# Cross-attention of a decoder block on one core: tile-outer order, unrolled, output summed in PSUM, mask added by PE, rope partners by DMA, bf16 P times V

## The reference

```
kv_c = kv @ W_kvc;  q_c = q @ W_dq                      # 64 and 96 columns
q_nope = q_c @ W_uq;  q_rope = rope(q_c @ W_qr)          # 16 heads, 128 and 64
k_nope = kv_c @ W_uk; v = kv_c @ W_uv; k_rope = rope(kv_c @ W_kr)
scores = (q_nope . k_nope + q_rope . k_rope) * scale     # per head, 64 x 64
scores = where(seg_id - 8 <= key <= seg_id, scores, -1e30)
x = layernorm(x + softmax(scores) @ v @ W_o)
rope([x1, x2]) = [x1*cos - x2*sin, x1*sin + x2*cos]      # halves of 32 each
```

## Time and profile before

| | |
|---|---|
| median of 3 runs | 1627.86 us (1627.15 to 1629.86) |
| the profiled execution's own time | 1630.34 us |
| its span | 1628.5 us |
| PE, DVE, ACT, POOL busy, of the span | 91%, 81%, 82%, 76% |
| self-attention | 0 to about 970 us |
| preparation of the cross-attention | about 970 to 1049 us |
| cross-attention | 1049.0 (first projection) to 1450.9 us (end of the last addition to X) |
| feed-forward | to the end |
| instructions | 54216 |

### The profile page before, as it was taken

How to read it: one execution, slowest core, us unless ns; L and a number is a source line. 1 busy time by engine, 2 the same in 40 slices (tenths; PEclk the granted TensorE clock), 3 DMA queues, 4 the chain that set the end, 5 groups by cost and what they waited for, 6 DMA issues and landing times. The chain is left out here.

```text
span 1628.5 us, 54216 instructions
## 1 busy us (share of the span) xinstructions
PE 1487.4 (91%) x20018; PEld 1083.8 (67%) x20018; DVE 1322.9 (81%) x2913; ACT 1334.4 (82%) x4174; POOL 1231.7 (76%) x1147
## 2 busy tenths in 40 slices
PE   6998999999999999999999968799999999845996
PEld 3666777777777777777777755366666666633664
DVE  3887777777777777777777778699999999967986
ACT  5877888888888888888888856599999999976664
POOL 5999888888898898898898846466666666611787
PEclk9999999999999999999999978999999999976999
DMA  6700000000000000000000002200000000000011
GB/s 222 191 2 15 16 3 15 16 15 3 15 15 3 16 15 5 13 15 15 3 15 3 3 2 68 86 3 2 0 0 0 0 0 0 0 1 0 14 39 53
DMA packets 27066, 36.92 MB, mean 23 GB/s; under 512 B 8288, under 2 KB 19872, under 8 KB 26848
## 3 DMA queue, kind: packets, MB, share of 16 engines
q1 hardware_dynamic: 26848, 33.99, 6.6%
HBM read 29.79 MB, written 4.19 MB: 21 GB/s over the span
## 5 line engine op out<-in xcount | busy, mean ns | idle before, releaser
L420 DVE SCALAR_TENSOR_TENSOR X<-projP,r,X 128x256 f32<-128x256 f32 x512 | 211.3, 476 | 2.5 <-PE projP L254 2.4
L234 PEld LDWEIGHTS svP<-W,xT 128*128 128x128 bf16 x3072 | 182.7, 98 | 31.4 <-issue 1.4
L205 PE MATMUL qkssP<-xT,W 128*128 128x512 bf16 x768 | 190.4, 384 | 13.5 <-POOL W L485 11.1
L480 POOL TENSOR_TENSOR y_sql<-y_sq 128x512 bf16<-128x512 f32 x128 | 133.0, 1039 | 80.5 <-ACT y_sq L321 80.1
L234 PE MATMUL svP<-W,xT 128*128 128x128 bf16 x3072 | 192.9, 219 | 0.7 <-issue 0.7
L205 PE MATMUL kP<-xT,W 128*128 128x512 bf16 x768 | 188.4, 382 | 0.0
L254 PE MATMUL projP<-W,y 128*128 128x256 bf16 x1024 | 177.1, 275 | 3.2 <-POOL yl L480 3.2
L943 ACT ACTIVATE x_probs<-x_scores,x_ntop 128x64 f32<-128x64 f32 x512 | 170.0, 335 | 7.4 <-DVE x_ntop L985 7.4
L336 ACT ACTIVATE probs<-scores,ntop 128x64 f32<-128x64 f32 x512 | 170.5, 339 | 1.9 <-DVE ntop L410 1.9
L1008 POOL TENSOR_TENSOR x_probs<-x_probs,x_inv 128x512 f32<-128x512 f32 x64 | 66.7, 1042 | 107.9 <-DVE x_inv L968 107.9
L480 POOL TENSOR_TENSOR k_sql<-k_sq 128x512 bf16<-128x512 f32 x128 | 133.1, 1040 | 19.8 <-ACT k_sq L341 19.2
(11 more groups left out here) (190 smaller groups left out, 4829.1 us busy)
## 6 DMA issues: line engine op xcount, KB each, us to landing
w_stage<-in_wqkvp SPq DMA_DIRECT2D x16, 512.0 KB, 3.5
x_stage<-in_xT SPq DMA_DIRECT2D x8, 512.0 KB, 3.6
X<-in_x SPq DMA_DIRECT2D x1, 4096.0 KB, 17.2
x_stage<-in_ctxT SPq DMA_DIRECT2D x8, 512.0 KB, 3.6
out<-X SPq DMA_DIRECT2D x8, 512.0 KB, 2.9
okv<-in_L_xattn_W_o SPq DMA_DIRECT2D x1, 2048.0 KB, 11.7
okv<-in_wgT SPq DMA_DIRECT2D x1, 1024.0 KB, 4.9
okv<-in_wuT SPq DMA_DIRECT2D x1, 1024.0 KB, 7.2
```

Source lines behind the costliest of these rows:

```text
L205: last = nc.tensor.matmul(dst[:, :], weight(parity, u, i, c), xT[:, z, c, tok], start=(c == 0 and k == 0), stop=(c == CC - 1 and k == 2))
L234: last = nc.tensor.matmul(svP[:, b * D:(b + 1) * D], xT[:, u, c, t * TILE + b * P:t * TILE + (b + 1) * P], weight(parity, z, 2, c), start= ...
L420: last = nc.vector.scalar_tensor_tensor(acc, projP[:, b * C:(b + 1) * C], r[:, PB + b:PB + b + 1], acc, ALU.mult, ALU.add)
L480: return nc.gpsimd.tensor_tensor(dst[:, :], src[:, :], high(src, slice(None), 0, TILE), ALU.subtract)
```

## The change

Seven things in the cross-attention change together.

1. Order: the tile is outside and the head pair inside (`m // HP`, `m % HP`), and all 64 slots are written out. The lags are now 3 (scores, exp), 4 (transposes), 5 (P times V) and 7 (projection).
2. Output: the projection of a tile's eight head pairs is summed in PSUM, so X is added to once a tile. The layer norm's statistics of the tile before follow, one block a slot.
3. Mask: it is kept in bf16, and PE adds it to the scores by a product with a bf16 identity. DVE takes the maximum from PSUM, and exp reads PSUM.
4. Rope: only the rope block is projected. DVE multiplies it by sin into `turn`, four DMAs bring each quarter of 32 partitions to its partner's place (`turned`), DVE multiplies the block by cos in PSUM, and the sum goes to `qh`, from PSUM and SBUF. There are two PSUM buffers for it.
5. Output's layout: ACT copies the output once into `oA`, and four DMAs bring its halves together in `oB`.
6. P times V: V and P are split into bf16 parts, and three bf16 passes take the place of the f32 product. DVE forms P's low part; in the preparation it forms V's.
7. Around it: `qh` has three buffers instead of two, the three feed-forward weight loads are issued in slots 8 to 10, the weight sums run in slots 64 to 66 on ACT, and the context's tokens are ordered within a tile as the values need it.

```diff
-                    for k in range(3):
...
-                            last = nc.tensor.matmul(qP[k][:, :], at(WQ[:, u, :, k], g), qc[:, z, j * TILE:(j + 1) * TILE],
+                    nc.tensor.matmul(sP[:, :], identb[:, :], mask[:, tile * BT:(tile + 1) * BT, :].rearrange("p b t -> p (b t)"),
+                                     start=True, stop=False)
...
+                if has(n, 0):
+                    tile, g = n // HP, n % HP
+                    for k, dst, done in ((1, ropeP[n % 2], s_ropeP), (0, latP, s_latP)):
+                        if k == 1:
+                            wait(pe, s_qh, n - 1)
+                        else:
+                            wait(pe, s_lat, n)
...
+                            last = nc.tensor.matmul(dst[:, :], WQ[:, u, g, k], qc[:, z, tile * TILE:(tile + 1) * TILE], start=(i == 0), stop=(i == 2))
...
+                            last = nc.tensor.matmul(oP[:, b * P:(b + 1) * P], KV[:, u, m // HP * PB + b, :], (pth, ptl)[z][:, m % 2, b * P:(b + 1) * P],
+                                                    start=(i == 0), stop=(i == 2))
...
+                            last = nc.tensor.matmul(projP[:, b * C:(b + 1) * C], o_part, WB[:, z, g], start=(g == 0 and b % 2 == 0 and i == 0),
+                                                    stop=(g == HP - 1 and b % 2 == 1 and i == 2))
```

The SP queue is new in each slot:

```diff
+            for n in range(N + PROJ_AT):
+                m = n - PV_AT - 1
+                if has(n, PV_AT + 1):
+                    wait(sp, s_oe, m + 1)
+                    wait(sp, s_proj, m - 1)
+                    for par in range(2):
+                        for i in range(2):
+                            sp.dma_start(oB[i * KVC:(i + 1) * KVC, m % 2, par * HT:(par + 1) * HT],
+                                         oA[par * KVC:(par + 1) * KVC, m % 2, i, :]).then_inc(s_ot[m % 2], 16)
+                if has(n, 0):
+                    wait(sp, s_turn, n + 1)
+                    wait(sp, s_qh, n - 1)
+                    half = R // 2
+                    for r in range(0, P, half):
+                        o = r + half if r % R == 0 else r - half
+                        sp.dma_start(turned[o:o + half, n % 2, :], turn[r:r + half, n % 2, :]).then_inc(s_swap[n % 2], 16)
+                if 8 <= n < 11:
+                    ffn_weights(n - 8, ("wgT", "wuT", "wdT")[n - 8])
```

ACT's and DVE's order in a slot is now: ACT exp (lag 3), copy of transposed P (4), latent copy (0), `oA` (5); DVE reciprocal (4), low part of P (5), maximum (3), sin product (0), sum into `qh` (1), cos product (0), X and statistics (7). In the preparation DVE gains, for each tile:

```diff
+                if 0 <= t < NT:
+                    dve.wait_ge(s_KV, t + 1)
+                    tk, own_ = tkP[:, 0:PB * KVC].rearrange("p (b k) -> p b k", b=PB), slice(t * PB, (t + 1) * PB)
+                    nc.vector.tensor_tensor(KV[0:T, 1, own_, 0:KVC], tk[0:T], KV[0:T, 0, own_, 0:KVC], ALU.subtract)
+                    nc.vector.tensor_tensor(KV[T:P, 1, own_, KVC:P], tk[T:P], KV[T:P, 0, own_, KVC:P], ALU.subtract).then_inc(s_KVl, 1)
```

More of the change, by code:

```diff
@@ L870, in _ @@
         @block.tensor
         def _(pe):
-            def slot(g, j, n, has):
-                if has(2):
-                    wait(pe, s_ql, n - 1)
-                    wait(pe, s_bias, n - 2)
-                    jj, s = (j - 2) % NT, j % 2
+            pe.wait_ge(s_ident, 1)
+            for n in range(N + PROJ_AT):
+                if has(n, S_AT):
+                    m = n - S_AT
+                    tile, s = m // HP, m % 3
+                    wait(pe, s_ql, m + 1)
+                    wait(pe, s_exp, m)
+                    nc.tensor.matmul(sP[:, :], identb[:, :], mask[:, tile * BT:(tile + 1) * BT, :].rearrange("p b t -> p (b t)"),
+                                     start=True, stop=False)
@@ L892, in slot @@
-                if has(3):
-                    wait(pe, s_norm, n - 2)
-                    wait(pe, s_pte, n - 3)
-                    for b in range(PB):
-                        last = nc.tensor.transpose(ptP[:, b * P:(b + 1) * P], probs[:, (j - 3) % 2, 2 * b:2 * b + 2, :].rearrange("p b s -> p (b s)"), ident[:, :])
-                    last.then_inc(s_pt, 1)
-                if has(4):
-                    wait(pe, s_pte, n - 3)
-                    wait(pe, s_oe, n - 4)
-                    jj = (j - 4) % NT
-                    for b in range(PB):
-                        last = nc.tensor.matmul(oP[:, b * P:(b + 1) * P], KV[:, jj * PB + b, :], probsT[:, b * P:(b + 1) * P], start=True, stop=True)
-                    last.then_inc(s_o, 1)
@@ L935, in slot @@
                                                     ACT.Copy, scale=SCALE)
                     last.then_inc(s_lat, 1)
-                if has(2):
-                    s = j % 2
-                    wait(act, s_top, n - 1)
-                    wait(act, s_inv, n - 2)
-                    wait(act, s_pt, n - 3)
-                    for b in range(BT):
-                        last = nc.scalar.activation(probs[:, s, b, :], scores[:, b, :], ACT.Exp, bias=ntop[:, b:b + 1], accum_out=total[:, b:b + 1])
-                    last.then_inc(s_exp, 1)
@@ L995, in slot @@
                     for i in range(2):
                         rows = slice(i * R, (i + 1) * R)
-                        last = nc.vector.tensor_tensor(qh[KVC:P, j % 2, :, i, :], turn[rows, 0], turn[rows, 1], ALU.add)
+                        last = nc.vector.tensor_tensor(qh[KVC:P, m % 3, :, i, :], by_token(ropeP[m % 2][rows, :]), by_token(turned[rows, m % 2]), ALU.add)
                     last.then_inc(s_qh, 1)
-            slots(dve, slot, HP, lags=7)
+                if has(n, 0):
+                    wait(dve, s_turn, n + 1)
+                    rope = by_token(ropeP[n % 2][:, :])
+                    nc.vector.tensor_tensor(rope, rope, tabs[:, 0, :].unsqueeze(1).to_broadcast([P, BT, T]), ALU.mult).then_inc(s_cos, 1)
@@ new lines, in _ @@
+                if has(n, PROJ_AT):
+                    m = n - PROJ_AT
+                    tile, g = m // HP, m % HP
+                    if g == HP - 1:
+                        wait(dve, s_proj, m + 1)
+                        acc = X[:, tile * PB:(tile + 1) * PB, :]
+                        nc.vector.tensor_tensor(acc, projP[:, :].rearrange("p (b c) -> p b c", b=PB), acc, ALU.add).then_inc(s_acc, 1)
+                    if tile >= 1 and 1 <= g < 1 + PB:
+                        wait(dve, s_acc, tile)
+                        next_norm.statistics((tile - 1) * PB + g - 1)
@@ L1301 @@
     swap = np.concatenate([np.arange(R // 2, R), np.arange(R // 2)])
-    W_qr, W_kr = np.asarray(inputs["L0_xattn_W_qr"]), np.asarray(inputs["L0_xattn_W_kr"])
-    arrays["qrs"] = W_qr.reshape(QC, H, R)[:, :, swap].reshape(QC, H * R)
+    W_kr = np.asarray(inputs["L0_xattn_W_kr"])
     arrays["wkr"] = np.concatenate([W_kr, W_kr[:, swap]], axis=1)
```

263 lines of the change are left out of this document (145 added, 118 removed).

## The result

The changed kernel takes 1607.9 us (median of 4 runs, 1605.0 to 1608.5), the kernel before on the same chip 1628.9 (1627.2 to 1631.9). The ratio is 0.9863 (0.9846 to 0.9881): 21 us faster, where 50 were forecast. The profiled executions have spans of 1605.6 and 1628.5. Their difference of 22.9 comes from the main stretch.

The account below looks back on a forecast made before the run. DVE and ACT, both 98% busy and in order, were taken to bound the kernel. Main stretch -47 (5.1 us a slot), drain -3, preparation +1, table load -1 gave -50: 1578 us for the median, range 1556 to 1610.

Parts of the forecast that it names:

- I take 0.50, nearer to the first: SP's queue in cross-attention: 0.50 us an issue, between 0.47 and 0.62, so eight issues take 4.0 us a slot.
- rival 1: Cross-attention: SP sets the pace through slow issues and landing, 5.2 to 5.6 us a slot, 1603 us at 5.5; chance 0.25.
- so unrolling gains nothing. Nor does it cost: Cross-attention's unrolled slots: no gain, as the loop showed no gap, and no cost, as self-attention is unrolled already.
- the forecast's 5.1 a slot: Cross-attention slot: ACT's 4.86 plus 0.06 for the X addition and 0.18 for handovers; ends 4.75 and 5.6 us.
- loop (b): Cross-attention's wait cycle through SP's oB and rope issues, landing, DVE and ACT: 14.3 us over three slots, 4.8 each.
- DVE, forecast 4.44: DVE's work per cross-attention slot: 4.44 us, 5.13 if the additions into qh are still held up, likely 4.5.
- ACT, 4.54 to 4.86: ACT's work per cross-attention slot: 4.86 us, or 4.54 if exps reading PSUM are cheaper.
- PE, 4.73: PE's work per cross-attention slot: 4.73 us, with six projections, the mask product and P times V in three bf16 passes.
- Rival 2: Cross-attention: everything packs well, exps are cheaper and PE's 4.73 binds; 4.8 us a slot, 1559 us; chance 0.13.
- Landing, 2.1: SBUF-to-SBUF DMAs in cross-attention: 2.1 us to land, with ends of zero and 3.8.
- Rival 4: Cross-attention: slower, the swap's late landing delays the addition into qh; 1671 us at a landing of 7.5; chance 0.06.
- Drain, forecast 30.5: From the last rope product to the last X addition: 30.5 us against 33.7, so -3, between -8 and +3.

Follow-up runs that it names:

- e5: Changed kernel with rope partners in adjacent rows, so two DMAs of 64 rows replace four of 32; 1574.2 us, ratio 0.9643.
- e1: Changed kernel with the same eight DMAs a slot, each carrying an eighth of its columns, so part of the computation is left out; 1599.7 us.
- e2: Changed kernel with the four rope DMAs a slot left out, so the rope is not computed; 1558.3 us.
- e12: Changed kernel without the rope DMAs and without the output's DMAs, so part of the computation is left out; 1553.9 us.
- e3: Changed kernel with the output's four DMAs once for two slots, 128 KB each, behind the rope DMAs, projection 8 slots behind; 1694.1 us, ratio 1.040.
- e6: Changed kernel with only the order of SP's two groups turned, rope DMAs before the output's; 1683.8 us, ratio 1.032.
- e8: Changed kernel with the output's four DMAs once for two slots, ahead of the rope DMAs, projection 9 slots behind; 1587.9 us, ratio 0.9721.

## Why the prediction was wrong

The failing step: "I take 0.50, nearer to the first, because a rope copy has 32 rows and tabs 128: 4.0." Neither the rows nor the bytes set the price of an issue (e5, e1). It is 0.64 from start to start, 5.1 a slot, and the long issues add 0.38: 5.49, which is above all other terms. With it the queue has no room and rival 1 holds. The time lies inside the stated 1556 to 1610, at its upper end, but not by the forecast's mechanism.

The 0.38 belongs to a second step: "so unrolling gains nothing. Nor does it cost". The self-attention, which was to show this, has no full queue of issues beside it. Over 63 slots 0.38 is 24 us, and the main stretch missed its forecast by 24.5. With SP at 5.1 the forecast's 5.1 a slot could have come out, for a wrong reason; that is an estimate from these rows, for no run has the eight issues without the loads.

Rival 1's numbers, 5.5 a slot and 1603 us, stand beside 5.45 and 1608, but that is partly luck. It came to 5.2 to 5.6 by loop (b) with slow issues and a landing of up to 3.8. The landing was 2.0, at which loop (b) gives (12.2 + 0.9 + 2.0) / 3 = 5.0. What filled the slot were SP's issues themselves, the long ones among them.

Point by point:

- DVE, forecast 4.44 (likely 4.5): 4.41 in e2. ACT, 4.54 to 4.86: 4.49, the lower end. oA took 0.60 (0.49 from start to start); an exp takes 0.29 from start to start instead of 0.33. PE, 4.73: 4.58. POOL, 3.92: 197.0 / 240 x 4.65 = 3.82.
- The slot of these: I took ACT's upper end and 0.24 for handovers and the X addition, 5.1. e12 shows 4.65. So there were two errors of opposite sign, +0.45 on the engines and -1.49 on SP's 4.0. Rival 2's 1559 stands near e2's 1558, in part by luck: its slot was 4.8 where e2's is 4.65, and e2's drain took 36.0 us, 1.7 more than before, where the sum had about 3 less.
- Landing, 2.1: 2.0 and 2.1. Right, and of no weight. The estimate of 2.15 that the prediction drew from the Trainium skill (DMA: Bandwidth & Descriptors, Anatomy of one DMA) is given there for DMAs issued from GpSimd; those of SP came near it. Rival 4 has the swap on the path by a late landing. The swap is on the path, but through the queue. Versions slower than before did appear, e3 and e6, by another wait: DVE waited for the partners only 6.2 and 10.0 us there, and GpSimd for the output 92.6 and 125.2.
- Drain, forecast 30.5 from the last product, measured 34.05. (Before it was 34.3 from the same product; the prediction set 30.5 against 33.7 from the product behind it, so its -3 should have been -3.8.) The last exp ended 17.5 after the product (18.0 forecast). From there to the end of the last oA it took 6.9 instead of 4.7: the last transposes stood in PE's queue behind P times V of the slot before, which waited for its low part, and PE was at a granted clock of 0.72 in 1411 to 1417. From oA to the addition it was 8.5, where the forecast had 4.1 + 1.0 + 1.5 = 6.6. The difference is a wait of SP: its last four issues went only at 1419.95, 2.0 after oA, because they waited for the projection of two slots earlier, which frees their buffer in oB. The rows: the clock's window; SP's last four issues, and SP's waits for the projection in 1396 to 1425 (us, times, longest); ACT's last oA and the last addition.

```profile
1411.00:1417.00 6.00, 4.54 (x38) 4.04 (x38) 1.92 (x4) 4.13 (x8) 2.04 (x2) 0.72 0.19 46
```

```profile
1419.95 2.38 SPq L893 DMA_DIRECT2D oB<-oA  x4
```

```profile
SPq L42 <- PE xprojP L958: 3.7, 4, 1.5
```

```profile
1417.37 0.60 ACT L992 ACTIVATE oA<-xoP 128x512 f32<-128x512 f32 x1 [1.47 <-PE xoP L939]
...
1426.44 1.23 DVE L1048 TENSOR_TENSOR X<-xprojP,X 128x1024 f32<-128x1024 f32 x1 [10.31 <-PE xprojP L958]
```

- Start, forecast 0 (+1 and -1): -0.5. That unrolling costs nothing held for PE, which is 97% busy in e12, but not beside SP's full queue (above).
- Account: -22.5 instead of -47 in the main stretch, -0.25 instead of -3 in the drain, the rest -0.15 instead of 0.

The Trainium skill (DMA: Bandwidth & Descriptors, Rules for kernel authors) advises one transfer of 128 partitions instead of two of half, for the sake of the DMA engines. No run here has just that pair. The nearest, two DMAs of 64 rows for four of 32, goes the same way, 1574 against 1608 us, but for another reason: bytes and DMA engines had room (DMA share 0.41), the queue that issues had not.

What stays open: how a load of code holds up an issue, and whether it does. The two coincide, and the loads follow PE's instructions and not SP's issues (e12), so SP's long issues come beside loads of what by that count is PE's code. What speaks for it: the load goes on where SP issues nothing. The trial would be a looped form with the eight issues, which no run has.

## What to carry to other kernels

Count a queue that only issues DMAs as an engine with a slot sum of its own, and price its issue from a burst, at the upper bound where that comes near the other sums (here 5.0 beside 4.9). Unrolled code is itself loaded by DMA: where such a queue is full, look whether its long issues fall on the loads. Replacing engine work by many small DMAs pays only while the count fits. If it doesn't, first make two DMAs carry what four carried, by laying out rows so that partners are strided neighbours. When two groups share such a queue, the more urgent one goes first only if the other has a slot of slack to give; lengthen the lag and add a buffer with it.

## What the runs showed that was not expected

- A DMA issue from SP took 590 to 597 ns in the median, 0.64 us from start to start, for 32 or 64 rows and 8 to 128 KB (e1, the changed kernel, e5); with 128 KB in two pieces a row 616 to 633 ns (e3, e8). At the kernel's start it had been 0.43.
- In the changed kernel's steady part, each of 17 issues of over 0.85 us lay on a load of 16 KB of code. The loads came once per 249 to 257 matmuls and weight loads of PE in nine runs, in e12 without any issue of SP.
- SBUF to SBUF a DMA of 64 KB landed after 1.9 us at least and 2.0 to 2.1 in the median, one of 8 KB after 1.8 in the median. One of 128 KB took 2.1 with whole rows (e5) and 2.4 with two pieces a row (e3, e8).
- Exchanging two groups of issues on a queue that was full cost 76 us (e6 against the changed kernel, each with its own runs of before: 1.0324 against 0.9863).
